# A conv-and-attention block on one core: second attention, adding the exponentials with accumulating transfers

## The reference, cut to what matters

```python
qk = einsum('bhqd,bhkd->bhqk', q, k)
qe = einsum('bhqd,qkd->bhqk', q, embeddings)
weights = softmax((qk + qe) / sqrt(d_head), axis=-1)
output = einsum('bhqk,bhkd->bhqd', weights, v)      # added to t afterwards
```

## Time and profile before

| | us |
|---|---|
| median of 3 runs | 2847.14 |
| lowest and highest | 2841.78, 2848.37 |
| the profiled execution's own time | 2855.66 |
| its span, first to last instruction | 2853.8 |
| granted TensorE clock, mean over the span | 0.941 |

### The profile page before, as it was taken

How to read it: one execution, slowest core, us unless ns; L and a number is a source line. 1 busy time by engine, 2 the same in 40 slices (tenths; PEclk the granted TensorE clock), 3 DMA queues, 4 the chain that set the end, 5 groups by cost and what they waited for, 6 DMA issues and landing times. The chain is left out here.

```text
span 2853.8 us, 47289 instructions
## 1 busy us (share of the span) xinstructions
PE 2481.0 (87%) x18516; PEld 817.5 (29%) x18516; DVE 1991.5 (70%) x3075; ACT 1402.8 (49%) x2548; POOL 1967.8 (69%) x763
## 2 busy tenths in 40 slices
PE   7899999999999999968988999999999999651255
PEld 2564222222222222235552222222222222240144
DVE  4475787787787787647886777877778777277134
ACT  3345555555555555523335565665656656440012
POOL 3114788888888888844446888888888888630763
PEclk9999999999999999989999999999999999775568
DMA  4994222322222322039764321223212230350337
GB/s 80 238 237 137 49 50 49 76 67 49 53 49 55 80 57 53 9 134 308 231 216 116 74 64 49 64 71 90 64 49 64 71 75 16 102 180 9 96 121 248
DMA packets 236267, 278.16 MB, mean 97 GB/s; under 512 B 65392, under 2 KB 171376, under 8 KB 232842
## 3 DMA queue, kind: packets, MB, share of 16 engines
q1 hardware_dynamic: 225548, 249.89, 32.3%
q0 software_dynamic: 6144, 16.85, 1.9%
q10 hardware_dynamic: 4352, 8.39, 0.8%
HBM read 165.17 MB, written 110.67 MB: 97 GB/s over the span
## 5 line engine op out<-in xcount | busy, mean ns | idle before, releaser
L854 POOL TENSOR_TENSOR room_af<-room_af 128x2048 f32<-128x2048 f32 x160 | 725.6, 4535 | 163.6 <-ACT room_af L826 149.8
L1229 POOL TENSOR_TENSOR bias<-bias 128x2048 f32<-128x2048 f32 x160 | 724.3, 4527 | 153.3 <-ACT bias L1199 134.1
L826 ACT ACTIVATE room_af<-PS 128x512 f32<-128x512 f32 x1024 | 555.9, 594 | 396.3 <-PE PS L748 396.3
L1199 ACT ACTIVATE bias<-PS 128x512 f32<-128x512 f32 x1024 | 555.9, 594 | 376.2 <-PE PS L1123 373.8
L635 DVE CUSTOM_DVE_ANT_0 PS<-PS,bias 128x1024 f32<-128x1024 f32 x512 | 620.1, 1241 | 160.6 <-PE PS L623 142.6
L1004 DVE TENSOR_REDUCE row_min_kf<-PS 128x1 f32<-128x1024 f32 x512 | 601.9, 1220 | 107.2 <-PE PS L996 98.6
L1118 PE MATMUL PS<-stacks_kf 128*128 128x512 f16 x1024 | 339.2, 387 | 15.3 <-PEq L90 8.5
L741 PE MATMUL PS<-QS_af,KS_af 128*128 128x512 f16 x1024 | 334.5, 387 | 14.3 <-PEq L90 4.5
L774 PE MATMUL PS<-room_af,V_af 128*32 128x512 f32 x2048 | 272.7, 605 | 1.2 <-ACT room_af L826 1.2
L1143 PE MATMUL PS<-bias,V_kf 128*32 128x512 f32 x2048 | 272.8, 605 | 0.2 <-ACT bias L1199 0.2
L748 PE MATMUL PS<-turned_bias,eyes 64*32 64x512 f16 x4096 | 210.6, 388 | 0.0
(11 more groups left out here) (184 smaller groups left out, 3070.4 us busy)
## 6 DMA issues: line engine op xcount, KB each, us to landing
query_key_halves<-bias SPq DMA_DIRECT2D x32, 768.0 KB, 4.0
query_key_halves<-room_af SPq DMA_DIRECT2D x32, 512.0 KB
stacks_kf<-query_key_halves SPq DMA_DIRECT2D x64, 256.0 KB, 7.2
KS_af<-query_key_halves SPq DMA_DIRECT2D x48, 256.0 KB, 4.8
QS_af<-query_key_halves SPq DMA_DIRECT2D x48, 256.0 KB, 7.0
lows_kf<-query_key_halves SPq DMA_DIRECT2D x96, 128.0 KB
token_rows<-rows_t SPq DMA_DIRECT2D x16, 514.0 KB, 4.2
FT_t<-token_rows SPq DMA_DIRECT2D x16, 514.0 KB
```

The costliest lines, as they stand in the source:

```text
L826: nc.scalar.activation(prob[:, n % PR, head, :], score_ps[s % 3], ACT.Exp).then_inc(exps, 1)
L854: nc.gpsimd.tensor_tensor(acc[:, u % 2], so_far, prob[:, n % PR], ALU.add).then_inc(acc_ok, 1)
L1199: nc.scalar.activation(prob[:, n % PR, j, :], score_ps[s % 3], ACT.Exp, scale=-1.0 / (W1S * W1S)).then_inc(exps, 1)
L1229: nc.gpsimd.tensor_tensor(acc[:, u % 2], so_far, prob[:, n % PR], ALU.add).then_inc(acc_ok, 1)
```

## The change

- Key tile 0 of a unit is no longer written into the ring but straight into a new tile `sums` (two of them, for alternate units). It is weighed from there like the rest.
- Key tiles 1, 2 and 3 (MOVED = 3) are added to `sums` by accumulating transfers (`move_tile`): POOL issues a DMA of 128 x 2048 float32 with `accum_op=add`. Each waits for the one before to land. Tiles 1 and 2 are issued in steps 1 and 2; tile 3 in step 5, behind the add of tile 5.
- POOL adds tiles 4, 5, 6, 7 into a single `acc` with three adds in steps 5, 6 and 7, and adds `acc` to `sums` with a fourth in step 1 of the next unit (`add_sums`), ahead of which it waits for the three transfers. In step 1 the transfer of the next unit's tile 1 is issued ahead of `add_sums`.
- PE sums one part (`sums`) and not three, in step DEN = 4 of the next unit. The reciprocals follow from REC = 5, over the unit's end, and `finish` comes in step 3 of the second unit after.
- The ring has PR = 5 tiles for seven key tiles a unit. ACT waits for a tile's transfer (`moved`), or its add, before it writes the ring tile again.

```diff
-                PR = 4
-                o1, o2 = HG * CH * PR, HG * CH * (PR + 2)
-                acc = zf[:, o1:o2].rearrange("p (r j n) -> p r j n", r=2, j=HG)
+                PR = 5
+                o1, o2 = HG * CH * PR, HG * CH * (PR + 1)
+                acc = zf[:, o1:o2].rearrange("p (j n) -> p j n", j=HG)
+                sums = tile("sums", [P, 2, HG, CH], F32)
...
-                ADDS = KTU - 3
+                MOVED = 3
+                LASTS = 0
+                ADDS = KTU - 1 - MOVED - LASTS
+                STEPS = KTU - 1
+                def prob(n):
+                    u, kt = divmod(n, KTU)
+                    return sums[:, u % 2] if kt == 0 else ring[:, (u * STEPS + kt - 1) % PR]
...
-                DEN, REC, TAKE, FIN = 1, 2, 1, 5
+                DEN, REC, TAKE, FIN = 4, 5, 1, 3
...
-                                parts = [prob[:, (KTU * u + kt) % PR] for kt in range(ADDS + 1, KTU)] + [acc[:, u % 2]]
+                                parts = [prob(KTU * u + kt) for kt in range(KTU - LASTS, KTU)] + [sums[:, u % 2]]
...
+                                u, kt = divmod(n, KTU)
+                                if kt == 0 and j == 0 and u >= 2:
+                                    act.wait_ge(max_full, job_at[(u - 2, "den")] + 1)
+                                if kt >= 1 and j == 0 and u * STEPS + kt - 1 >= PR:
+                                    u, kt = divmod(u * STEPS + kt - 1 - PR, STEPS)
+                                    act.wait_ge(weighed, KTU * u + kt + 2)
+                                    if kt < MOVED:
+                                        act.wait_ge(moved, 16 * (MOVED * u + kt + 1))
+                                    elif kt + 1 < KTU - LASTS:
+                                        act.wait_ge(acc_ok, ADDS * u + max(kt - MOVED, 1))
...
+                            def move_tile(n):
+                                u, kt = divmod(n, KTU)
+                                pool.wait_ge(exps, HG * (n + 1))
+                                if kt == 1:
+                                    pool.wait_ge(weighed, KTU * u + 1)
+                                if MOVED * u + kt >= 2:
+                                    pool.wait_ge(moved, 16 * (MOVED * u + kt - 1))
+                                nc.gpsimd.dma_start(sums[:, u % 2].rearrange("p j n -> p (j n)"), prob(n).rearrange("p j n -> p (j n)"),
+                                                    accum_op=ALU.add).then_inc(moved, 16)
...
+                                first = kt == MOVED + 2
+                                done = ADDS * u + kt - MOVED - 2
+                                if done >= 1:
+                                    pool.wait_ge(acc_ok, done)
+                                nc.gpsimd.tensor_tensor(acc, prob(n - 1) if first else acc, prob(n), ALU.add).then_inc(acc_ok, 1)
+
+                            def add_sums(u):
+                                pool.wait_ge(moved, 16 * MOVED * (u + 1))
+                                pool.wait_ge(acc_ok, ADDS * (u + 1) - 1)
+                                nc.gpsimd.tensor_tensor(sums[:, u % 2], sums[:, u % 2], acc, ALU.add).then_inc(acc_ok, 1)
+
+                            LATE_ADD, SUMMED, BACK = KTU - LASTS - 1, 1, 2
+                            for n in range(NU * KTU + 2):
+                                u, kt = divmod(n, KTU)
+                                if n < NU * KTU and 1 <= kt <= 2:
+                                    move_tile(n)
+                                if n < NU * KTU and MOVED + 2 <= kt <= LATE_ADD:
+                                    add_tile(n)
+                                if n < NU * KTU and kt == MOVED + 2:
+                                    move_tile(n - 2)
+                                if kt == SUMMED and u >= 1:
+                                    add_sums(u - 1)
+                                if u < NU and kt == FIN and u >= BACK:
+                                    finish(u - BACK)
+                            for u in range(NU - BACK, NU):
+                                finish(u)
...
-                                u, piece = n // KTU - 1, n % KTU - REC
+                                u = n // KTU - 1
                                 if u >= 0 and n % KTU == DEN:
                                     take_sums(job_at[(u, "den")], u)
+                                u, piece = divmod(n - REC, KTU)
+                                u -= 1
```

More of the change, by code:

```diff
@@ L910, in attention_keys_first @@
                 max_row = tile("max_row", [HG * TT, 2, P], F16)
-                PR = 4
-                o1, o2 = HG * CH * PR, HG * CH * (PR + 2)
-                prob = zf[:, 0:o1].rearrange("p (r j n) -> p r j n", r=PR, j=HG)
-                acc = zf[:, o1:o2].rearrange("p (r j n) -> p r j n", r=2, j=HG)
+                PR = 5
+                o1, o2 = HG * CH * PR, HG * CH * (PR + 1)
+                ring = zf[:, 0:o1].rearrange("p (r j n) -> p r j n", r=PR, j=HG)
+                acc = zf[:, o1:o2].rearrange("p (j n) -> p j n", j=HG)
+                sums = tile("sums", [P, 2, HG, CH], F32)
                 rec = zf[:, o2:o2 + 2 * CH].rearrange("p (r n) -> p r n", r=2)
@@ L934, in attention_keys_first @@
                 LOADS = 16 * 14
-                ADDS = KTU - 3
+                MOVED = 3
[5 more added lines that the diff above has]
+                    return sums[:, u % 2] if kt == 0 else ring[:, (u * STEPS + kt - 1) % PR]
                 sems = [ssem(n) for n in ("stk0", "stk1", "v_in0", "v_in1", "x_in0", "x_in1", "out_st0", "out_st1", "m_in0",
                                           "m_in1", "emb_in", "high_in", "fill", "max_full", "max_read", "full", "exps", "weighed",
-                                          "acc_ok", "recd", "taken", "scaled", "fin")]
+                                          "acc_ok", "moved", "recd", "taken", "scaled", "fin")]
                 (stk0, stk1, v_in0, v_in1, x_in0, x_in1, out_st0, out_st1, m_in0, m_in1, emb_in, high_in, fill, max_full, max_read,
-                 full, exps, weighed, acc_ok, recd, taken, scaled, fin) = sems
+                 full, exps, weighed, acc_ok, moved, recd, taken, scaled, fin) = sems
                 stk, v_in, x_in, out_st, m_in = (stk0, stk1), (v_in0, v_in1), (x_in0, x_in1), (out_st0, out_st1), (m_in0, m_in1)
@@ L1144, in weigh @@
                                                             V[:, bb % 2, kt, (g * HG + j) * D:(g * HG + j + 1) * D],
-                                                            prob[:, n % PR, j, :], start=(kt == 0), stop=(kt == KTU - 1),
+                                                            prob(n)[:, j, :], start=(kt == 0), stop=(kt == KTU - 1),
                                                             skip_group_check=True)
@@ L1198, in _ @@
                                 act.wait_ge(full, s + 1)
-                                nc.scalar.activation(prob[:, n % PR, j, :], score_ps[s % 3], ACT.Exp,
+                                nc.scalar.activation(prob(n)[:, j, :], score_ps[s % 3], ACT.Exp,
                                                      scale=-1.0 / (W1S * W1S)).then_inc(exps, 1)
@@ L1218, in add_tile @@
                             def add_tile(n):
                                 u, kt = divmod(n, KTU)
-                                if kt == 0 or kt > ADDS:
-                                    return
                                 pool.wait_ge(exps, HG * (n + 1))
[L1224 to L1235, removed]
+                                first = kt == MOVED + 2
```

## The result

| | before | after |
|---|---|---|
| median, us | 2846.8 (4 runs) | 2942.0 (4 runs) |
| lowest and highest | 2841.8, 2848.4 | 2940.4, 2943.7 |
| profiled execution, us | 2855.7 | 2942.5 |
| its span | 2853.8 | 2940.7 |

The changed kernel is slower by 95 us: ratio 1.0338, 95% interval 1.032 to 1.0355. It lies 12 us above the range that was given, where a loss of 10 us was forecast. The sign of the forecast time was right; its size was not, and "faster" had been given nearly as much chance as "slower".

The account below looks back on a forecast made before the run. PE was taken as the bound, handing PSUM banks back and forth with ACT. Terms: -57 us PE, +25 ring, +35 beside loads, +7 end, +10 in all: 2857 us; own range 2823 to 2876, 80% range 2793 to 2930.

Parts of the forecast that it names:

- PE's term: Step with the sums: 8 matmuls for 24 save 1.85 us in each of 31 units, 57 us in all.
- POOL's chain: Exponentials of tile 5 to the end of `add_sums`: 21.1 us, just fitting when PE wants the sums; no slack.
- The ring's allowance of 6.6 us: Tile 3's transfer must land within 6.6 us of issue before ACT rewrites its slot; any excess is lost one for one.
- A transfer alone: An accumulating transfer with no loads beside it: 7.4 us from issue to landing, bounds 4.8 and 10.0.
- Tile 3: Its transfer overruns the ring's time by 0.8 us in 31 units, plus 2.5 beside loads in 14 transitions.
- Tiles 1 and 2 have far more room: Their transfers are issued near 7.9 and 13.4 us, wanted at 21.8 and 25.5; no cost unless over 9 us.
- The end: The last unit has nothing beside it; from its step 6 to the store 28.4 us for 21.5, 7 lost.
- Two reads: Likeliest case: an accumulating transfer pays for reading source and destination; 2857 us, from 2823 to 2876, chance 0.38.
- three passes: Rival: transfers pay three passes over the bytes, 10.0 us alone, also holding up POOL; 2956 us, chance 0.12.
- The quick case: Rival: transfers land within 6.6 us alone, little lost to loads; unit is PE's 27.86 us, 2797 in all, chance 0.35.
- A: Theory after the trace: loads meeting transfers, and tile 2 issued late, cause the waits; e1 under 2860, e10 2815 to 2845.

Follow-up runs that it names:

- e4: The kernel before, with PE summing acc alone and tiles 6 and 7 left out of the denominator: 2789.1 us, ratio 0.9794.
- e1: The changed kernel, with loads of queries and keys cut to an eighth of their columns from the third group of heads on: 2893.9 us, ratio 1.0164.
- e10: The changed kernel, with nearly all loads of the second attention cut to an eighth or a quarter, the residual's store kept: 2898.9 us, ratio 1.0143.
- e3: The changed kernel with a ring of six tiles (PR = 6) and not five: 2873.6 us, ratio 1.0094.
- e5: The changed kernel with two moved tiles (1 and 2), a ring of six and five POOL adds: 2870.4 us, ratio 1.0037 to the kernel before.
- e8: e5 with a ring of seven, no acc, and tile 2's transfer issued a step later, behind the add of tile 5: ratio 1.0035 to the kernel before.
- e2: The changed kernel, with the three accumulating transfers as plain copies of the same size: 2821.6 us, ratio 0.9912.

## Why the prediction was wrong

- **PE's term** was 57 us and is 44. The step with the sums shrank by 1.72 and not 1.85 us (e4), and the copy of the output, hidden under the sums before, costs 0.33 in step 1. That the copy stays in step 1 while the sums leave it was in the code, and it was not costed.
- **POOL's chain** fits, as worked out: step 4 loses nothing in the changed kernel. Its issues were taken at 1.32 us and measure 0.87, of which about 0.6 come between two operations, so it had more room than the zero that was given.
- **The ring's allowance of 6.6 us** was right: a transfer that lands in 7.0 lengthens the way into step 1 by 0.37 us (4.03 for 3.66).
- **A transfer alone** was forecast at 7.4 and takes 6.9 to 7.0; its bytes take 5.3 us of the engines, against the 5.2 of two reads.
- **Tile 3** was to lose 0.8 x 31 + 2.5 x 14 = 60 us and lost 59.2 in the changed kernel. That the two agree is in part luck. In the changed kernel it loses 45 us in the fifteen units where it meets loads or the residual's store; the forecast for such units was 14 x 3.3 = 46, but it had only the loads in view, and in seven of them it is the store that was issued just ahead (at 1961.03 us, tile 3 at 1961.8). In the other sixteen it loses 14 us, forecast as 0.8 each: 10 of them in the six that have an instruction packet beside them, which was in no sum, and 5 in the ten where it is alone.
- **The step that failed** is "Tiles 1 and 2 have far more room ... They cost nothing unless a transfer takes over 9 us". The condition was stated and its price was not put into the sum. The loads were weighed against tile 3 alone, whose bytes meet the loads' beginning, for up to 3.8 us. Tile 1 is issued into the middle of them, at T0 + 10 to T0 + 13, when nearly all loads are queued, and took 12.5 to 15.0 us in 13 of 15 such units, 5.5 to 8 more than alone. POOL waited for it, tile 2 left at T0 + 25 instead of T0 + 13.4, and step 7 lost 40 us, plus most of the 10 in step 0 with the slow clock. With the loads cut (e1) step 7 loses 9.9 and step 0 1.1.
- **The clock** was not in the sum. Behind most of the waits of over 2 us PE's next step took 4.2 to 5.5 us for 3.33, 17 us in step 2 over the stage. So of the 85 us between the forecast +10 and the measured +95, some 68 are steps 7, 0 and 2, and 13 are PE's term.
- **The end** was +7 and is +7.
- **The cases.** "Two reads" had the transfer right, and 2942 is outside its range of 2823 to 2876; the time was near that of "three passes" (2956), whose 10.0 us for a transfer alone is refuted by the 7.0. The quick case failed at its own point: 7.0 is over 6.6.
- Of my own second theories, A's numbers for e1 and e10 were too low by some 45 to 70 us, because it put all of tile 3's lateness down to the loads that were cut; and e3, e5 and e8 were each expected to be the last wait and were followed by another.

## What to carry to other kernels

Work given to the DMA engines is not free because their share is low: cost each transfer at its landing time beside what is queued when it is issued, and then cost what it holds up, the loads, which had 5 us to spare here, and the small transfers. Where transfers of two kinds share the engines, issue them in the gaps of each other: the same two transfers a unit gave +0.4% beside the loads and -0.8% behind them. A wait in an in-order queue belongs where the thing awaited is surely there, and a ring must hold a tile for the worst landing time, not the median.

## What the runs showed of the hardware

- An accumulating transfer of 1 MB from SBUF to SBUF lands in 6.9 to 7.0 us alone, a plain copy in 4.4 to 4.6 (e10, e2). The bytes keep the 16 engines busy for 5.3 us, the copy's for 2.8. POOL is held for 0.87 and 0.55 us by the issue.
- Issued among the loads of the next heads it lands in 12.5 to 15.0 us in 13 of the 15 units of the changed kernel that have loads, and as a copy (e2) in 8.1 to 12.9. The loads suffer alike: the values' megabyte lands in 15.2 us (median of 8), 8.9 before.
- SP's issue of a transfer slows beside it: the 1 KB transfers took a median of 0.57 us each to issue in the kernel before (at most 1.30), and 0.94 in e5 (at most 1.56).
- After PE had stood idle for 3.73 us its granted clock was 0.57 over the next 4 us, and the eight weighing matmuls took 1.93 us for 1.06.
- With one packet of 16 KB of the instruction queue in its course and nothing else, an accumulating megabyte took 8.2 to 8.7 us (six of e10's tile 3), and 6.9 to 7.0 without (ten of them); the same six and ten took 7.9 to 8.5 and 6.9 to 7.0 in the changed kernel. Whether the packet is the cause was not tested.
